# A fused gated cross-attention and expert block on one core: moved copies, router arithmetic in pieces, biases spread, first weight chunk by two queues

## The reference

```python
x = x + tanh(g_xattn) * attention(layernorm(x), ctx, ctx)    # x: (8, 128, 512); 32 query heads, 8 key heads of 128
#   q = ln(x) @ Wq ; k = ctx @ Wk ; v = ctx @ Wv ; rotary tables by position on q and k
#   softmax(q k^T / sqrt(128), masked) @ v @ Wo
h = layernorm(x)
ratio = mean|h[38:]| / mean|h[:38]|                          # one number for each batch element
scores = softmax(concat(h, ratio) @ gate_w + gate_b)         # three experts
w = two largest scores / their sum
e1, e2 = the two best experts of token 0 of each batch element
moe = w1 * expert[e1](h) + w2 * expert[e2](h)
#   expert e: act_e(h @ w1[e] + b1[e]) @ w2[e] + b2[e];  act = tanh, gelu, silu
x = x + tanh(g_ffn) * moe
```

## Time and profile before

| what | value |
|---|---|
| median of three executions | 711.09 us (710.73 to 711.72) |
| the profiled execution | 710.4 us |
| its span, first to last instruction | 708.7 us |
| outside the span | 1.7 us |
| granted TensorE clock, mean | 1.000 |
| PE busy | 691.0 us (98%) |
| DVE, POOL, ACT busy | 561.4, 401.6, 361.6 us |

### The profile page before, as it was taken

The page is one execution under the profiler, slowest core; times in us unless marked ns, Lnnn a source line. Parts: engine busy times, 40 slices in busy tenths (PEclk is TensorE's granted clock), DMA queues, the critical chain, the costliest instruction groups (busy, mean ns, idle before and its releaser), DMA issues.

```text
span 708.7 us, 11561 instructions
## 1 busy us (share of the span) xinstructions
PE 691.0 (98%) x3478; PEld 579.0 (82%) x3478; DVE 561.4 (79%) x950; ACT 361.6 (51%) x961; POOL 401.6 (57%) x345
## 2 busy tenths in 40 slices
PE   8999999999999999999999999999999988989997
PEld 6787887888888888888888888888888867768885
DVE  5688776887887888878878878888788977776885
ACT  5625534545555455455455554554555677554521
POOL 6689855666576676666666766666666654420000
PEclk9999999999999999999999999999999999999999
DMA  8997564322222221222212222212222422210001
GB/s 258 318 331 282 186 204 145 106 84 65 68 83 60 74 77 59 87 61 61 87 60 69 80 59 78 70 59 89 60 67 83 148 62 75 71 49 16 16 31 59
DMA packets 65967, 70.84 MB, mean 100 GB/s; under 512 B 8576, under 2 KB 42368, under 8 KB 65920
## 3 DMA queue, kind: packets, MB, share of 16 engines
q1 hardware_dynamic: 65536, 69.25, 30.9%
q0 software_dynamic: 384, 1.05, 0.5%
HBM read 51.40 MB, written 18.87 MB: 99 GB/s over the span
## 4 chain that ended last, share of the span: by engine, by line
PE 83%; DVE 8%; ACT 3%; DMA 3%; POOL 2%; issue 1%; SPq 0%; DVEq 0%; ACTq 0%; POOLq 0%
PE q L298 28%; PE y L288 27%; PE o L664 6%; PE s L646 5%; PE q L288 5%; PE pt L509 4%; PE s L648 2%; PE pt L288 2%; PE o L288 2%; DMA wraw<-in_L_xattn_Wk 1%; PE s L288 1%; PE s L509 1%; ACT prob L974 1%; DVE split L1269 1%; DVE scores L1547 1%
## 5 line engine op out<-in xcount | busy, mean ns | idle before, releaser
L288 PE MATMUL y<-big,split 128*128 128x512 f32 (+1 forms) x864 | 209.4, 392 | 4.0 <-DVE split L1269 3.9
L288 PEld LDWEIGHTS y<-big,split 128*128 128x128 f32 x864 | 161.2, 188 | 38.0 <-DVE split L1269 4.9
L298 PE MATMUL q<-xT_hi,big 128*128 128x512 f32 x512 | 175.2, 404 | 0.0
L1207 POOL TENSOR_TENSOR roped<-rot 128x512 f32<-128x512 f32 x58 | 75.1, 1294 | 101.6 <-DVE rot L1295 101.6
L974 ACT ACTIVATE prob<-scores,nmax 128x128 f32<-128x128 f32 x256 | 99.9, 391 | 24.5 <-DVE nmax L1424 24.5
L960 ACT ACTIVATE big<-roped 128x512 fp32r<-128x512 f32 x63 | 39.9, 634 | 141.4 <-POOL roped L1207 136.3
L298 PEld LDWEIGHTS q<-xT_hi,big 128*128 128x128 f32 x512 | 96.2, 188 | 19.0
L1221 POOL TENSOR_TENSOR prob<-prob,prec 128x512 f32<-128x512 f32 x64 | 66.6, 1040 | 64.0 <-DVE prec L1429 64.0
L298 PE MATMUL q<-xT_lo,big 128*128 128x512 f32 x256 | 99.6, 389 | 0.0
L1210 POOL TENSOR_TENSOR big<-roped,big 128x512 fp32r<-128x512 f32 x63 | 81.5, 1293 | 13.2 <-ACT big L960 13.2
L1199 POOL TENSOR_TENSOR big<-wraw,big 128x512 fp32r<-128x512 f32 x64 | 83.1, 1298 | 0.0
(11 more groups left out here) (198 smaller groups left out, 1276.6 us busy)
## 6 DMA issues: line engine op xcount, KB each, us to landing
wraw<-in_L_xattn_Wq SPq DMA_DIRECT2D x32, 256.0 KB, 3.0
wraw<-in_L_xattn_Wo SPq DMA_DIRECT2D x32, 256.0 KB, 2.9
kv<-k_scratch SPq DMA_DIRECT2D x64, 128.0 KB, 2.5
kv<-v_scratch SPq DMA_DIRECT2D x64, 128.0 KB, 2.8
v_scratch<-split SPq DMA_DIRECT2D x12, 512.0 KB, 4.1
wraw<-in_L_ffn_w SPq DMA_DIRECT2D x24, 256.0 KB, 3.0
k_scratch<-split SPq DMA_DIRECT2D x10, 512.0 KB, 4.0
k_scratch<-kv SPq DMA_DIRECT2D x6, 512.0 KB, 3.7
```

The lines of the kernel that those rows point to most:

```text
L288: mm = pe.matmul(bank_[:, :], stationary(s, c), moving(m, c), start=(c == 0 and n == 0), stop=(c == EC - 1 and n == 2))
L298: mm = pe.matmul(bank_[:, :].rearrange("p (b t) -> p b t", b=BH), weights[s][:, c, h * P:(h + 1) * P], source[m][:, half * BH:(half + 1) * ...
L1207: pool.tensor_tensor(roped[:, :], rot[:, 0, :], rot[:, 1, :], ALU.add).then_inc(q_roped, 1)
```

## The change

Five things are changed.

1. The drain. `output_hi` is taken out of `drain_unit` and put right behind the exponentials, ahead of `norm_row`, `h_hi_`, `w_expert_hi` and `sum_abs`; `sum_abs` moves behind `drain_unit`.
2. The router's arithmetic. `ranked_weights` is cut after its third step; the rest (`weight_sums`), `slot_weights` and its end (`bias_weights`) stand further back, among the items' steps.
3. The biases. The 24 calls of `bias` are spread anew over the loop of items: fewer ahead of `pair_select`, more behind `add_slot`, none in the last pass.
4. The start. Weight chunk 0 is issued by ACT's queue, and its high half is made in two halves of 256 columns by ACT and DVE; its low half comes before the arithmetic on the positions. The positions are handed over transposed (by the host, from the inputs) and read as rows of 32 bytes.
5. TensorE no longer waits for the identity before its zero products (the wait stands behind `first_values`), and there are nine of them.

```diff
-BLANKS = 8
+BLANKS = 9
@@ SP
             for k in range(EC):
                 c_load(k)
-                w_load(k, w_chunks[k]).then_inc(w_in[k % NW], 16)
-                if k == 0:
-                    sp.dma_start(posi[:, :], pos.rearrange("b s -> s b"), allow_slow_non_contiguous=True
-                                 ).then_inc(pos_in, 16)
+                if k >= 1:
+                    w_load(k, w_chunks[k]).then_inc(w_in[k % NW], 16)
+                else:
+                    sp.dma_start(posi[:, :], pos).then_inc(pos_in, 16)
@@ PE
-            pe.wait_ge(ident_ok, 2)
...
+                    if c == 0:
+                        pe.wait_ge(w0_half, 1)
...
             first_values()
+            pe.wait_ge(ident_ok, 2)
@@ ACT, start
-            for k in range(EC):
+            act.dma_start(wraw[:, 0, :], w_chunks[0]).then_inc(w_in[0], 16)
+            c_hi_(0)
+            act.wait_ge(w_in[0], 16)
+            act.activation(w_target(0)[0][0][:, 0, 0:256], wraw[:, 0, 0:256], ACT.Copy).then_inc(w0_half, 1)
+            act.wait_ge(w_hi, 1)
+            for k in range(1, EC):
@@ ACT, drain_unit
-                output_hi(UNITS + b - LAG_Y)
-                if b < LAG_Y - 1:
-                    w_expert_hi(W_D + (0, 1, 2, 3, 5, 7)[b])
+                w_expert_hi(W_D + (0, 1, 2, 3, 5, 7)[b])
@@ DVE, start
+            dve.wait_ge(w_in[0], 16)
+            dve.tensor_copy(w_target(0)[0][0][:, 0, 256:512], wraw[:, 0, 256:512]).then_inc(w_hi, 1)
             c_lo_(0)
+            dve.wait_ge(w0_half, 1)
+            w_lo_(0)
             dve.wait_ge(pos_in, 16)
@@ DVE, items
             ranked_weights()
             dense_z(5)
-            slot_weights()
             pair_select(2)
-            pair_select(3)
             pair_add(4)
             pair_lo_(0)
+            pair_select(3)
             pair_add(5)
             pair_lo_(1)
+            weight_sums()
             pair_select(4)
+            pair_lo_(2)
+            slot_weights()
+            pair_lo_(3)
             add_slot(0)
-            pair_lo_(2)
+            bias_weights()
...
             for j in range(CHOSEN + 2, 2 * B):
+                later = 0 if j == 2 * B - 1 else 2 if B + 2 <= j < B + 6 else 1
                 pair_add(j)
                 pair_lo_(j - 1)
-                bias(done)
-                bias(done + 1)
+                if j < 2 * B - 1:
+                    bias(done)
+                    done += 1
+                    if j < B + 2:
+                        bias(done)
+                        done += 1
+                        later = 0
                 pair_select(j)
                 add_slot(j - 2)
-                if B <= j - 2 < B + 4:
-                    bias(done + 2)
-                done += 3 if B <= j - 2 < B + 4 else 2
+                for n in range(done, done + later):
+                    bias(n)
+                done += later
```

More of the change, by code:

```diff
@@ L165, in build @@
         w_in = [sem(f"w_in{k}") for k in range(NW)]
-        w_hi, w_lo = sem("w_hi"), sem("w_lo")
+        w_hi, w_lo, w0_half = sem("w_hi"), sem("w_lo"), sem("w0_half")
         pool_const, ident_ok, blank_ok = sem("pool_const"), sem("ident_ok"), sem("blank_ok")
@@ L1057, in _ @@
             groups(act, unit)
+            output_hi(UNITS - 7)
             drain_unit(0)
             exponentials(UNITS - 5, 1, B)
+            output_hi(UNITS - 6)
             drain_unit(1)
             exponentials(UNITS - 4, 0, B)
+            output_hi(UNITS - 5)
             drain_unit(2)
             exponentials(UNITS - 3, 1, B)
+            output_hi(UNITS - 4)
             norm_row(1, 0)
+            drain_unit(3)
             sum_abs(0)
-            drain_unit(3)
             exponentials(UNITS - 2, 0, B)
+            output_hi(UNITS - 3)
+            h_hi_(0)
             norm_row(1, 1)
-            h_hi_(0)
             w_expert_hi(W_D + 4)
+            drain_unit(4)
             sum_abs(1)
-            drain_unit(4)
             exponentials(UNITS - 1, 1, B)
             norm_row(1, 2)
+            output_hi(UNITS - 2)
             h_hi_(1)
+            norm_row(1, 3)
             w_expert_hi(W_D + 6)
-            norm_row(1, 3)
-            sum_abs(2)
             drain_unit(5)
             norm_row(1, 4)
+            sum_abs(2)
+            sum_abs(3)
             w_expert_hi(W_D + 8)
-            sum_abs(3)
             h_hi_(2)
-            drain_unit(6)
+            output_hi(UNITS - 1)
             h_hi_(3)
@@ L1296, in rotate, with w_lo_ @@
                                   ).then_inc(done, 1)
+            def w_lo_(n):
+                buf, c = w_target(n)
+                dve.wait_ge(w_hi, n + 1)
+                subtract_hi(buf[1][:, c, :], wraw[:, n % NW, :], buf[0][:, c, :], w_lo)
+            dve.wait_ge(w_in[0], 16)
+            dve.tensor_copy(w_target(0)[0][0][:, 0, 256:512], wraw[:, 0, 256:512]).then_inc(w_hi, 1)
             c_lo_(0)
+            dve.wait_ge(w0_half, 1)
+            w_lo_(0)
             dve.wait_ge(pos_in, 16)
@@ L1309, in _ @@
                               ).then_inc(pos_ok, 1)
-            def w_lo_(n):
-                buf, c = w_target(n)
-                dve.wait_ge(w_hi, n + 1)
-                subtract_hi(buf[1][:, c, :], wraw[:, n % NW, :], buf[0][:, c, :], w_lo)
-            for k in range(EC):
-                if k >= 1:
-                    c_lo_(k)
+            for k in range(1, EC):
+                c_lo_(k)
                 w_lo_(k)
@@ L1652, in ranked_weights, with weight_sums @@
                 settle()
+            def weight_sums():
                 tt(top, weight1, weight2, ALU.add)
@@ L1676, in slot_weights, with bias_weights @@
                 settle()
+            def bias_weights():
                 tt(parts[:, 0:2, :], weight[:, :, :], out_of[:, :, :], ALU.mult)
@@ L1717, in _ @@
             dense_z(5)
-            slot_weights()
             pair_select(2)
-            pair_select(3)
             pair_add(4)
             pair_lo_(0)
+            pair_select(3)
             pair_add(5)
             pair_lo_(1)
+            weight_sums()
             pair_select(4)
+            pair_lo_(2)
+            slot_weights()
+            pair_lo_(3)
             add_slot(0)
-            pair_lo_(2)
+            bias_weights()
             pair_select(5)
             add_slot(1)
-            pair_lo_(3)
             add_slot(2)
@@ L1733, in _ @@
             add_slot(3)
-            done = 0
+            bias(0)
+            bias(1)
+            done = 2
             for j in range(CHOSEN + 2, 2 * B):
+                later = 0 if j == 2 * B - 1 else 2 if B + 2 <= j < B + 6 else 1
                 pair_add(j)
                 pair_lo_(j - 1)
-                bias(done)
-                bias(done + 1)
+                if j < 2 * B - 1:
[5 more added lines that the diff above has]
+                        later = 0
                 pair_select(j)
                 add_slot(j - 2)
-                if B <= j - 2 < B + 4:
-                    bias(done + 2)
-                done += 3 if B <= j - 2 < B + 4 else 2
+                for n in range(done, done + later):
+                    bias(n)
+                done += later
             assert done == B * NX
@@ L1766 @@
             continue
-        a = np.ascontiguousarray(inputs[name])
+        a = np.ascontiguousarray(inputs[name].T if name == "pos_BxS2" else inputs[name])
         arrays[f"in_{name}"] = a
```

## The result

| | before | after |
|---|---|---|
| median, same chip | 711.04 us (4 executions, 710.73 to 711.72) | 702.17 us (4 executions, 700.67 to 703.39) |
| the profiled execution, its span | 710.4, 708.7 us | 702.05, 700.3 us |
| PE busy | 691.0 us (98%) | 691.8 us (99%) |

The ratio is 0.9873 (95% interval 0.9852 to 0.9894): 9.0 us faster. Forecast were 701.2 us, in a range of 698.9 to 705.0.

What follows compares the result with a forecast made beforehand. TensorE, busy 98% of the span, was taken as the bound, so only its waits could be won. 1.2 + 3.4 + 4.2 + 1.1 = 9.9 us off gave a median of 701.2 us, range 698.9 to 705.0.

Steps and rivals of the forecast that it cites:

- The start: First 24.6 us: earlier zero products and two waits gone or mostly gone, 1.2 us, bounds 0 and 1.7.
- the zero products: At the start: they begin at some 1.4 instead of 2.10 us and end earlier, gaining 0.3 us.
- the two waits: At the start: 0.41 us before the fifth value tile goes, 0.42 us for a rotary table mostly goes.
- The drain: 551 to 601 us: three y waits, 4.6 us, go; less 0.95 and 0.2 us, 3.4 us gained.
- no y weight load waits over 0.5 us: Drain: a sign that would show the forecast right, y's weight loads no longer waiting for DVE's low half of o.
- low bound of 2.2 us: Drain: the gain left if the layer norm chain is met twice more by a POOL split of 1.29 us.
- Router and items: Behind the router: waits of 1.22 and 2.75 us go, plus 0.2 us of slow restart, 4.2 us; bounds 2.4 and 4.4.
- The last pass: Last pass: without two biases the selection comes earlier and TensorE's wait before it goes, 1.1 us; bounds 0.6 to 1.3.
- the drain gives its gain back: Rival, drain: the layer norm chain sets the pace, gain 2.2 us or less, 702.4 to 703.4 us; chance 15%.
- no new wait stood among the items: Rival, items: another wait replaces the 2.75 us, router and items bring 2.4 us, 703.0 us; chance 11%.
- the start brings less than expected but not nothing: Rival, start: the start brings nothing, 702.4 us; chance 7%.
- The rival of the slow clock: Rival, start: clock stays low for 20 us or more; with 60 slow products 713.1 us; chance 3%.

Runs made afterwards that it cites:

- e2_drain_alone: The kernel before with only ACT's new order in the drain; 708.42 us, ratio 0.9947.
- e12_short_drain: The changed kernel with two of POOL's weight splits in the drain made on 32 of 512 columns only; 701.55 us, ratio 0.9858.
- e3_router_alone: The kernel before with only the router's arithmetic in four pieces and the biases spread; 704.68 us, ratio 0.9907.
- e11_short7: The kernel before with the last eight low halves of the expert weights made by POOL on 32 of 512 columns only; 707.48 us, ratio 0.9944.
- e9_chain: The changed kernel with four swaps of order in the drain, on DVE, ACT and POOL; 701.46 us, ratio 0.986.

## Why the prediction was right

**The start, 1.2 us expected.** The trace showed 1.7, the mean of eight traces 0.9: that the trace shows more than forecast is luck of that execution. Right: the beginning of the zero products at 1.39 us, piece 7 sooner (14.87 us, though not near 14), both waits gone in this trace. Too high: the zero products, taken at 0.3 us. The first real product starts 0.12 us earlier here and 0.18 to 0.29 us in the other seven traces, since it waits for ACT's half of chunk 0, which stands behind piece 0. And the two waits were counted as gone or mostly gone, while the one for the rotary table stands in four of the eight traces with the new start and the one before the fifth value tile in three. How the rise of the clock goes with the start of the products is not decided. With the same start at 1.39 us the nine zero products took 4.21 us in the changed kernel (all at the lower level) and 3.77 us in its repeat (the last ones at the higher); by the traces' record of the clock the rise lies between 4.50 and 7.31 us in the eight traces with the new start (mean 5.9), and between 5.84 and 7.20 in the six with the old one (mean 6.6). By the Trainium skill (TensorE: Matmul & The Clock Gate, What's actually happening), which calls the gate's observation free-running, the rise varies from execution to execution; these traces agree.

**The drain, 3.4 us expected, 3.05 measured** (3.04 in `e2_drain_alone`). The three waits of y went, and the meeting of a negated mean with a split came on TensorE's path as named, 1.00 us (0.95 expected), worth 0.9 us by `e12_short_drain`. It was not one more, as the prediction says: the one of before went from its own step. Missing from the sum was the last power, which stood behind a split and left the last transposes waiting 1.06 us where they had waited 0.35. The sign "no y weight load waits over 0.5 us" failed with the 0.93 us at 588.20. The prediction's low bound of 2.2 us should read 2.0 by its own terms (4.6 - 2 x 1.29).

**Router and items, 4.2 expected, 4.12 measured** in `e3_router_alone`. The dense bias began at 617.37 there (617.6 expected). The mechanism, splits that hold waiting operations, is shown by `e11_short7`, which gets the same gain (4.0 us) without moving an instruction. The rule of the Trainium skill (SBUF — State Buffer, Who interferes with whom), that a DVE instruction with two SBUF inputs and a GpSimd instruction that reads SBUF shut each other out, agrees: the operations concerned have two such inputs.

**The last pass, 1.1 expected, 1.07 measured.** From the transposes at 641.66 (before) and 634.38 (after) to the last matmul at 704.95 and 696.60 the distance shrank from 63.29 to 62.22 us: 1.07.

**The sum.** The terms as measured, 0.9 + 3.05 + 4.1 + 1.1, make 9.15 us; the medians of 711.04 and 702.17 us are 8.9 apart, and 9.9 were forecast. The forecast was 1.0 us low. Of it 0.3 us is the start, 0.35 the drain, 0.1 the router and items; the other 0.2 us is less than four executions between 700.67 and 703.39 us can tell. The half-rate stretch, which the prediction did not foresee, is not the missing term: by the mean clock it comes before the change as well (35 of 51 executions, 5 of 9 after it), and the executions at a mean clock of 0.999 or 1.000 alone are 710.39 - 701.75 = 8.6 us apart. It does part the two traces, since the one before has none. Their spans differ by 8.4 us: 1.7 at the start, 3.05 in the drain, 2.5 from there to the second item's transposes (4.2 less 1.7 lost at the lower clock), 1.1 in the last pass. In that pair a start 0.8 us better than its mean and a stretch at the lower clock pull against each other.

Of the rivals, "the drain gives its gain back" came a third of the way (3.05 between 3.4 and 2.2); no new wait stood among the items; the start brings less than expected but not nothing. The rival of the slow clock was wrong on the place: nowhere did the lower level last 20 us at the start (the latest rise is at 7.31 us), but the clock fell later in the kernel, for 3.4 us.

## What to carry to other kernels

Short vector operations on a few columns that wait for one another should not stand beside long GpSimd operations (here 128x512 splits of 1.27 us): each wait can cost the rest of one. Look at a chain's operations one by one when they are moved: an operation that gets its operand earlier may land exactly beside the next long one, as in `e9_chain`, and nothing is gained. Ask of a trace whether its mean clock is that of the median execution before subtracting microseconds from it. And take a gain of under a microsecond from several traces: one trace put the start at 1.7 us, eight at 0.9.

## What the runs showed of the hardware that was not expected

- TensorE's granted clock fell from 2.4 to 1.2 GHz for some 3.4 us in the middle of kernels that were 98% busy: behind waits of 1.5 and 2.7 us, and behind 18 small products with next to no wait (some 1.7 us of TensorE's time each). By the mean clock 35 of 51 executions of the kernel before had at least one, 5 of 9 of the changed kernel; with 50 small products in a row all 12 had, for 10.2 us in the trace. Why it comes in one execution and not in the next is not shown, and neither spreading the small products nor full products between them kept it away.
- Eight vector operations on 8 columns took 1.15, 3.13 or 4.16 us with 0, 3 or 4 full GpSimd splits beside them, 0.7 to 1.0 us for each. A negated mean on one column took 0.15 us alone and 0.95 to 1.23 us beside one.
- With 4 bytes an element, the load of 4 KB of positions put some 870 packets more into the first 20 us and delayed what was queued behind it by 0.9 us on average (piece 7 at 15.31 to 16.47 us in five traces, 14.23 to 15.33 in nine without it).
- Two loads of 256 KB issued at once by two queues landed later than the first in one queue: piece 0 reached ACT at 4.27 to 4.48 us in eight traces, instead of 3.27 to 3.71 in six.
